# Attention output: one PSUM bank for both units of a pair, normalised between two VectorE transposes; the third group's evacuation on VectorE and four early score steps

## The chip, the cores and the metric

The kernel runs on one core of one Trainium2 chip. The metric is the device time of one execution in microseconds (us), lower is better; the time given is the median of several executions. Below, PE is TensorE, ACT is ScalarE, DVE is VectorE, POOL is GpSimd and SP is the queue that issues the DMAs.

## What is computed

A block on x of shape (2, 1024, 128): half a mixture-of-experts feed-forward (FFN), causal attention with 8 heads of 8 channels and l2-normalised queries and keys, and the same half FFN again.

```python
x = x + 0.5 * ffn(layernorm(x))     # 8 experts of 256 hidden, all computed for each token, summed, times a gate
x = x + attention(layernorm(x))
x = x + 0.5 * ffn(layernorm(x))

# attention
q, k, v = split(xn @ w_qkv)                       # (128, 192); 8 heads x 8 channels each
sim  = (l2norm(q) @ l2norm(k).T) * 8.0            # causal
o    = softmax(sim) @ v                           # (2, 8, 1024, 8)
out  = concat_heads(o) @ w_out                    # (64, 128)
```

## The kernel before

The 2,048 tokens are 4 groups of 512. Each engine has its own instruction list, written out by hand, and semaphores join them; nothing is reordered by a scheduler. There are three phases. Layer 0 (an FFN) handles the groups one after the other, 16 chunks of hidden units per group: per chunk PE makes three matmuls `up` (L443 to L449) and three `down` (L461 to L466), ACT a gelu (L765, L768), DVE the split into a high and a low part (L932, L934). Beside the chunks it makes the layer norm, q, k and v of the groups that are finished. Attention follows, then layer 1 (a second FFN).

**Attention** is 80 steps `s` in 40 quad steps `k` (a quad step is one block of keys for four heads; its two steps are two heads each). Per step PE makes the scores (L570) into one of `S_SETS` = 3 pairs of PSUM banks, ACT the exponentials (L778) into one of 8 slots, and POOL masks diagonal blocks (L1254). Per quad step PE then multiplies the probabilities with the values, `pv` (L591), `PV_LAG` = 3 quad steps later. So PE's list for quad step k is: scores 2k, scores 2k+1, pv(k-3), then at most one **job**. A score step waits until the exponentials that used its banks three steps before are done. Most steps hold 2x512 columns; the last of each unit holds 2x256.

A **unit** is (batch, query group, quad): 8 units of 3, 3, 7, 7, 3, 3, 7, 7 quad steps. `pv` adds a unit up in one PSUM bank, `output_bank(u)` = 7 or 6 in turn, as 4 heads x 32 rows (8 channels, the sum of the probabilities from a column of ones in `v_ones`, zeros) by 512 queries. The other of the two banks serves the **jobs** (`fill(n)` on PE writes it, `empty(n)` on DVE reads it): for each unit "rows" (DVE copies the bank to `oT`, L1076, PE transposes it in 4 tiles, L622, DVE divides by the sums, L1107 and L1109); for each second unit "features" (transposes back, L625, copy L1114) and "project" (times `w_out`, L628, added to x, L1118); and, for the fourth group, which the attention phase prepares itself, "ln" (L611), "qk" (L614), "v" (L617), "q_stack" and "k_stack" (L548). The next unit's first `pv` waits until the jobs in its bank are emptied.

The third group (p = 2) is prepared at the end of layer 0: in PE's chunks 12 and 13 of the last group stand the first score step, transposes (L414) and the products `qkv_products` (L538); ACT copies the second group's keys (L741), makes `xf` (L714), then the squares (L724) and the copies of q, k and v (L729, L734) and the FFN output `yT` (L788). The last unit's "rows", "features" and "project" stand in chunks 2, 4 and 6 of layer 1's first group.

## Time and profile before

| | |
|---|---|
| median of 3 executions | 298.76 us (298.69 to 298.80) |
| the profiled execution | 298.09 us, its span in the trace 296.4 us |
| PE matmuls busy | 280.2 us (95%) |
| ACT busy | 226.1 us (76%) |
| DVE busy | 216.8 us (73%) |
| POOL busy | 87.0 us (29%) |

Busy time is the union of an engine's instructions; matmuls are pipelined, so "busy" on PE holds overlaps, and the distance from one start to the next is what a matmul costs. Attention lies between about 118 and 197 us of the span, layer 0 before it and layer 1 behind it.

### The profile page before, as it was taken

What the parts mean: (1) busy time and instruction counts of PE and PEld (TensorE: products, weight loads), DVE (VectorE), ACT (ScalarE), POOL (GpSimd) and SP (SyncE); (2) the same over time, 40 slices, a digit from 0 to 9 for tenths busy, and PEclk for the clock granted to TensorE, in tenths of its full rate; (3) what the DMA queues carried; (4) which work ended last, traced back from release to release, by engine and by line L of the source; (5) the groups of instructions that cost most, each with busy time, mean ns of one, the idle gap of its engine ahead of it and who ended that gap; (6) DMA issues with size and microseconds to landing.
All of it is one profiled execution on the core that took longest, in us unless ns stands there. A gap on an engine that the chain in (4) does not pass through costs nothing.

```text
span 296.4 us, 5295 instructions
## 1 busy us (share of the span) xinstructions
PE 280.2 (95%) x1707; PEld 195.6 (66%) x1707; DVE 216.8 (73%) x567; ACT 226.1 (76%) x349; POOL 87.0 (29%) x151
## 2 busy tenths in 40 slices
PE   8898999999989988699989989899999999999995
PEld 8585788788778875143414433268888888888882
DVE  6799988979988886873593451148679797888675
ACT  2875877777877787999798899976677677687672
POOL 5333204204860680542137303212030310310010
PEclk9999999999999999899999999999999999999998
DMA  5710000000000000000000000000000100100101
GB/s 165 237 46 1 0 1 2 0 1 2 0 1 0 3 1 0 2 0 2 0 3 2 1 2 0 2 0 0 2 0 2 35 2 0 35 0 0 35 3 35
DMA packets 8060, 4.66 MB, mean 16 GB/s; under 512 B 642, under 2 KB 8036, under 8 KB 8036
## 3 DMA queue, kind: packets, MB, share of 16 engines
q1 hardware_dynamic: 8036, 4.35, 4.9%
q8 instruction: 13, 0.21, 0.3%
q14 instruction: 11, 0.09, 0.1%
HBM read 3.30 MB, written 1.05 MB: 15 GB/s over the span
## 4 chain that ended last, share of the span: by engine, by line
PE 69%; POOL 9%; ACT 7%; DVE 6%; issue 6%; SPq 1%; DMA 1%; DVEq 0%; POOLq 0%; ACTq 0%
PE ps L591 9%; PE ps L466 8%; PE ps L461 8%; PE ps L443 8%; PE ps L449 8%; PE ps L446 8%; PE ps L464 7%; ACT probs L778 3%; PE ps L570 3%; POOL rstd L1176 2%; PE ps L423 2%; PE ps L628 1%; PE ps L548 1%; PE ps L622 1%; DVE h_lo L934 1%
## 5 line engine op out<-in xcount | busy, mean ns | idle before, releaser
L765 ACT ACTIVATE h<-ps,cols 128x512 f32<-128x512 f32 x128 | 88.0, 690 | 50.5 <-PE ps L449 45.4
L934 DVE TENSOR_TENSOR h_lo<-h,h_hi 128x512 fp32r<-128x512 f32 x128 | 92.0, 724 | 29.0 <-ACT h_hi L768 26.0
L778 ACT ACTIVATE probs<-ps 128x1024 f32<-128x1024 f32 (+1 forms) x80 | 68.6, 962 | 6.1 <-PE ps L570 5.9
L461 PE MATMUL ps<-h_hi,w_hi 128*128 128x512 f32 x128 | 53.0, 414 | 0.3 <-DVE h_hi L932 0.3
L466 PE MATMUL ps<-h_lo,w_hi 128*128 128x512 f32 x128 | 50.9, 398 | 1.8 <-DVE h_lo L934 1.8
L443 PE MATMUL ps<-xT_hi,w_hi 128*128 128x512 f32 (+1 forms) x128 | 50.7, 396 | 0.3 <-ACT xT_hi L839 0.3
L449 PE MATMUL ps<-xT_lo,w_hi 128*128 128x512 f32 (+1 forms) x128 | 50.1, 391 | 0.0
L464 PE MATMUL ps<-h_hi,w_lo 128*128 128x512 f32 x128 | 50.0, 391 | 0.0
L446 PE MATMUL ps<-xT_hi,w_lo 128*128 128x512 f32 (+1 forms) x128 | 49.9, 390 | 0.0
L768 ACT ACTIVATE h_hi<-ps,cols 128x512 fp32r<-128x512 f32 x72 | 49.1, 682 | 0.0
L1254 POOL TENSOR_SCALAR_AFFINE_SELECT probs<-probs 128x256 f32<-128x256 f32 x64 | 26.4, 435 | 54.5 <-ACT probs L778 53.6
L591 PE MATMUL ps<-probs,v_ones 128*32 128x512 f32 (+3 forms) x384 | 40.2, 511 | 0.9 <-DVE x_sb L1118 0.5
L466 PEld LDWEIGHTS ps<-h_lo,w_hi 128*128 128x128 f32 x128 | 24.0, 188 | 9.9 <-DVE h_lo L934 4.8
L932 DVE CAST h_hi<-h 128x512 fp32r<-128x512 f32 x56 | 24.8, 443 | 7.1 <-ACT h L765 6.2
L443 PEld LDWEIGHTS ps<-xT_hi,w_hi 128*128 128x128 f32 x128 | 24.0, 188 | 5.8 <-ACT xT_hi L839 0.5
L461 PEld LDWEIGHTS ps<-h_hi,w_hi 128*128 128x128 f32 x128 | 24.1, 188 | 5.5 <-DVE h_hi L932 1.5
L449 PEld LDWEIGHTS ps<-xT_lo,w_hi 128*128 128x128 f32 x128 | 24.0, 188 | 5.5 <-DVE xT_lo L1129 0.2
L446 PEld LDWEIGHTS ps<-xT_hi,w_lo 128*128 128x128 f32 x128 | 24.0, 188 | 5.1
L464 PEld LDWEIGHTS ps<-h_hi,w_lo 128*128 128x128 f32 x128 | 24.2, 189 | 3.8
L570 PE MATMUL ps<-qT,kT 32*128 32x512 f16 (+3 forms) x192 | 20.0, 335 | 3.5 <-ACT probs L778 3.1
L570 PEld LDWEIGHTS ps<-qT,kT 32*128 32x128 f16 x192 | 5.7, 92 | 20.9 <-ACT probs L778 12.3
L1176 POOL TENSOR_TENSOR gate_rms<-gate_ms,neg_half 128x4 f32<-128x4 f32 x8 | 9.6, 1201 | 29.0 <-DVE gate_ms L899 29.0
(127 smaller groups left out, 301.4 us busy)
## 6 DMA issues: line engine op xcount, KB each, us to landing
w_raw<-in_L_ffn_w SPq DMA_DIRECT2D x8, 256.0 KB, 4.3
x_sb<-in_L_attn_x SPq DMA_DIRECT2D x3, 256.0 KB, 7.3
out_x<-x_sb SPq DMA_DIRECT2D x3, 256.0 KB, 2.3
x_sb<-in_L_attn_x SPq DMA_DIRECT2D x2, 128.0 KB, 2.1
out_x<-x_sb SPq DMA_DIRECT2D x2, 128.0 KB, 1.8
wqkv_sb<-in_L_attn_w_qkv SPq DMA_DIRECT2D x1, 96.0 KB, 6.7
wout_sb<-in_L_attn_w_out SPq DMA_DIRECT2D x1, 32.0 KB, 3.4
small<-in_L_ffn_b SPq DMA_DIRECT2D x1, 8.0 KB
```

The lines of the kernel that those rows point to most:

```text
L443: pe.matmul(bank, w1_hi[:, w], xT_hi[:, cols_g], start=True, stop=False)
L446: pe.matmul(bank, w1_lo[:, w], xT_hi[:, cols_g], start=False, stop=False)
L449: pe.matmul(bank, w1_hi[:, w], xT_lo[:, cols_g], start=False, stop=True).then_inc(up_done, 1)
L461: pe.matmul(y, w2_hi[:, w], h_hi[:, c % RING, :], start=(c == 0), stop=False)
L464: pe.matmul(y, w2_lo[:, w], h_hi[:, c % RING, :], start=False, stop=False)
L466: pe.matmul(y, w2_hi[:, w], h_lo[:, c % RING, :], start=False, stop=(c == CHUNKS - 1)).then_inc(down_done, 1)
L570: m = pe.matmul(ps[:, 2 * (s % S_SETS) + hd, at:at + width], kT[rows, st["quad"], k0:k0 + P], qT[rows, st["quad"], qc:qc + width], start=T ...
L591: m = pe.matmul(ps[ROW * j:ROW * j + ROW, bank, q0:q0 + width], v_ones[:, SEQ // P * st["b"] + kt, 4 * st["quad"] + j, :], probs[:, (s + j ...
L765: first = nc.scalar.activation(h[:, slot, :], ps[:, BANK_H + slot, :], ACT.Gelu, bias=bias)
L768: nc.scalar.activation(h_hi[:, slot, :], ps[:, BANK_H + slot, :], ACT.Gelu, bias=bias).then_inc(gelu_done, 1)
L778: nc.scalar.activation(probs[:, s % P_SLOTS, :, 0:width], ps[:, bank:bank + 2, 0:width], ACT.Exp, scale=SCALE).then_inc(exp_done, 1)
L934: dve.tensor_tensor(h_lo[:, slot, :], h[:, slot, :], h_hi[:, slot, :].bitcast(f32), ALU.subtract).then_inc(split_done, 1)
```

## The change

- **One bank for both units of a pair.** `v_ones` puts the second quad's channels and ones 16 columns further on (`SPREAD`), with zeros elsewhere, so both quads' `pv` add up in one bank: 16 rows for each of the 8 heads. There are 4 pairs instead of 8 units: quad steps 0-5, 6-19, 20-25, 26-39.
- **Normalising on DVE alone.** `output(pair)` makes a DVE transpose of 32x32 blocks out of the bank into `o_blocks`, a reciprocal, a product into `o_scaled`, and a second transpose into `o_feat`. The jobs "rows" and "features" are gone from PE. `wout_sb` gets 128 rows (zeros between the heads), loaded by 8 DMAs instead of 1, after a memset on POOL.
- **Jobs.** "project" is cut into two halves of 2 tiles; "qk" and "v" become two "qkv" jobs of 2 tiles and 192 columns. Their quad steps are set anew. In layer 1's first group "project" alone is left, in chunk 3.
- **The third group's evacuation**: copies of k of the second group, of q, k and v of the third, and the squares, move from ACT to DVE. In groups 1 and 2 ACT copies the values by four instructions instead of two.
- **Four early steps**: score steps 1, 2 and 3 stand in chunks 13, 14 and 15 of layer 0's last group (step 0 was in chunk 12 already); `score_set` gives steps 0 to 3 the banks 0 to 3 by turns. ACT makes the first two exponentials before `yT`.

```diff
-        u0, u1, u2, u3 = last_quad[0:4]
-        jobs = [(u0 + 1, "rows", 0), (u0 + 2, "q_stack", LAST - 1), (u0 + 3, "k_stack", LAST - 1),
-                (u1 + 1, "rows", 1), (u1 + 2, "features", 1), (u1 + 3, "project", 1),
-                (u1 + 4, "ln", LAST), (u1 + 5, "qk", LAST), (u1 + 6, "v", LAST), (u2 + 4, "rows", 2),
-                (u2 + 5, "q_stack", LAST), (u2 + 6, "k_stack", LAST)]
...
-        jobs.append((last_quad[4] + 2, "ffn_ln", 0))
...
-        jobs += [(quad_steps, "rows", u), (quad_steps, "features", u), (quad_steps, "project", u)]
+        jobs = [(q1, "ln", LAST), (q1 + 1, "project", (0, 0)), (q1 + 2, "project", (0, 1)),
+                (q1 + 5, "qkv", 0), (q1 + 6, "qkv", 1), (q1 + 7, "q_stack", LAST - 1), (q1 + 8, "k_stack", LAST - 1),
+                (q1 + 12, "q_stack", LAST), (q2 + 1, "k_stack", LAST),
+                (q2 + 4, "project", (1, 0)), (q2 + 5, "project", (1, 1)),
+                (q3 + 1, "project", (2, 0)), (q3 + 2, "project", (2, 1)), (q3 + 5, "ffn_ln", 0),
+                (quad_steps, "project", (pairs - 1, None))]
...
-        def output_bank(u):
-            return 7 - u % 2
+        def score_set(s):
+
+            return s % 2 if s < 4 else (s - 2) % S_SETS
+
+        def set_reader(s):
+
+            return s - 2 if s in (2, 3) else None if s == 4 or s < 2 else s - S_SETS
+
+        def output_bank(pair):
+            return 7 - pair % 2
...
-            sp.dma_start(wout_sb[:, :], w_out).then_inc(wout_in, 16)
+            sp.wait_ge(const_self, 6)
+            for head in range(HEADS):
+                row = ROW * (head % 4) + SPREAD * (head // 4)
+                sp.dma_start(wout_sb[row:row + HEAD_DIM, :], w_out[HEAD_DIM * head:HEAD_DIM * head + HEAD_DIM, :]).then_inc(wout_in, 16)
...
-                    if layer == 1 and first and c in (2, 4, 6):
-                        fill(len(jobs) - 4 + c // 2)
+                    if layer == 1 and first and c == 3:
+                        fill(len(jobs) - 1)
...
+                    if operands and last and c >= at["att_qkv"]:
+                        if c == at["att_qkv"]:
+                            pe.wait_ge(gelu_done, CHUNKS * GROUPS)
+                        scores(1 + c - at["att_qkv"])
...
-                if s >= S_SETS:
-                    pe.wait_ge(exp_done, s - S_SETS + 1)
+                if set_reader(s) is not None:
+                    pe.wait_ge(exp_done, set_reader(s) + 1)
...
+                opens, closes = st["first"] and st["quad"] == 0, st["last"] and st["quad"] == QUADS - 1
+                if opens and pair == 0:
                     pe.wait_ge(kT_done, LAST - 1)
-                if st["first"] and st["unit"] == 1:
+                if opens and pair == 1:
                     pe.wait_ge(resid, GROUP_TILES * GROUPS)
-                if st["first"] and st["unit"] > 1:
+                if opens and pair > 1:
                     pe.wait_ge(job_emptied, sum(at < k for at, *_ in jobs))
                 if st["diagonal"]:
...
-                                      start=(st["first"] and n == 0), stop=(st["last"] and n == len(st["item"]) - 1))
+                                      start=(opens and n == 0), stop=(closes and n == len(st["item"]) - 1))
...
                     pe.wait_ge(job_emptied, n)
+                if n == 0 or pair_of_job(n) != pair_of_job(n - 1):
+                    pe.wait_ge(o_copied, pair_of_job(n))
                 tiles = [slice(P * i, P * i + P) for i in range(GROUP_TILES)]
                 if kind in ("q_stack", "k_stack"):
                     pe.wait_ge(stack_done, 2 * arg + 2)
...
+                elif kind == "qkv":
+                    for i in halves[arg]:
+                        m = pe.matmul(bank[:, 192 * (i % 2):192 * (i % 2) + 192], xf[:, ATT, tiles[i]], wqkv_sb[:, :],
+                                      start=True, stop=True)
                 elif kind == "project":
-                    for tile in tiles:
+                    pair, half = arg
+                    pe.wait_ge(o_ready, pair + 1)
+                    for tile in tiles if half is None else [tiles[i] for i in halves[half]]:
...
-                        square_qk(g - 1)
-                        copy_qkv(g - 1)
+                        exp_scores(1)
...
+            def copy_k(p):
+                dve.wait_ge(stack_t, p + 1)
+                dve.tensor_copy(kT[:, :, GROUP * p:GROUP * p + GROUP],
+                                ps[:, BANK_KT, :].bitcast(f16).rearrange("p (a q) -> p a q", a=QUADS)).then_inc(kT_done, 1)
+
+            def copy_qkv(p):
+                dve.wait_ge(qkv_mm, p + 1)
+                dve.wait_ge(qkn_done, 2 * p)
+                halves_qkv = [ps[:, bank, 0:384].rearrange("p (t c) -> p t c", t=2) for bank in qkv_banks(p)]
+                for half, qkv in enumerate(halves_qkv):
+                    dve.tensor_copy(qk_raw[:, 2 * half:2 * half + 2, :], qkv[:, :, 0:2 * INNER])
+                for half, qkv in enumerate(halves_qkv):
+                    for quad in range(QUADS):
+                        last = dve.tensor_copy(v_of(slice(4 * p + 2 * half, 4 * p + 2 * half + 2), quad), v_columns(qkv, quad))
+                last.then_inc(qkv_copied, 1)
...
+                        copy_k(g - 2)
+                        copy_qkv(g - 1)
+                        own_squares(g - 1)
...
-                            copy_o(len(units) - 1)
-                        if c in (2, 4, 6):
-                            empty(len(jobs) - 4 + c // 2)
-                        if c == 7:
+                            output(pairs - 1)
+                        if c == 3:
...
-            def copy_o(u):
-                dve.wait_ge(pv_done, quads_until_unit[u])
-                if u:
-                    dve.wait_ge(job_filled, job_number["rows", u - 1] + 1)
-                dve.tensor_copy(oT[:, :], ps[:, output_bank(u), :]).then_inc(o_copied, 1)
+            def output(pair):
+
+                dve.wait_ge(pv_done, quads_until_unit[QUADS * pair + QUADS - 1])
+                dve.transpose(o_blocks[:, :, :].rearrange("p b r -> p (b r)"), ps[:, output_bank(pair), :]).then_inc(o_copied, 1)
+                dve.wait_ge(o_copied, pair + 1)
+                split_rows = o_blocks[:, :, :].rearrange("p b (q s) -> p b q s", q=QUADS)
+                dve.reciprocal(rden[:, :, :], split_rows[:, :, :, HEAD_DIM]).then_inc(rden_done, 1)
+                dve.wait_ge(rden_done, pair + 1)
+                if pair == 0:
+                    dve.wait_ge(o_zero, 1)
+                dve.tensor_tensor(o_scaled[:, :, :].rearrange("p b (q s) -> p b q s", q=QUADS)[:, :, :, 0:HEAD_DIM],
+                                  split_rows[:, :, :, 0:HEAD_DIM],
+                                  rden[:, :, :].unsqueeze(3).to_broadcast([P, BLOCKS, QUADS, HEAD_DIM]),
+                                  ALU.mult).then_inc(o_scaled_done, 1)
+                dve.wait_ge(o_scaled_done, pair + 1)
+                if pair:
+                    dve.wait_ge(job_filled, job_number["project", (pair - 1, 1)] + 1)
+                dve.transpose(o_feat[:, :], o_scaled[:, :, :].rearrange("p b r -> p (b r)")).then_inc(o_ready, 1)
 
...
+                elif kind == "qkv":
+                    dve.wait_ge(qkn_done, 2 * LAST)
+                    qkv = bank[:, 0:384].rearrange("p (t c) -> p t c", t=2)
+                    t0 = GROUP_TILES * LAST + halves[arg][0]
+                    dve.tensor_copy(qk_raw[:, halves[arg][0]:halves[arg][1] + 1, :], qkv[:, :, 0:2 * INNER])
+                    for quad in range(QUADS):
+                        last = dve.tensor_copy(v_of(slice(t0, t0 + 2), quad), v_columns(qkv, quad))
+                    last.then_inc(job_emptied, 1)
```

PE in layer 0's last group, from chunk 13's `down` on (L538 are the products for q, k and v, L570 before and L602 after the scores, L477 and L505 the transposes of `yT`). Before:

```order
L538 MATMUL ps<-wqkv_sb,xf 128x192 [waits qT_done,xf_done_att]
L538 MATMUL ps<-wqkv_sb,xf 128x192 x3
L461 MATMUL ps<-h_hi,w2_hi 128x512 [waits gelu_done]
L464 MATMUL ps<-h_hi,w2_lo 128x512
L466 MATMUL ps<-h_lo,w2_hi 128x512 [waits split_done]
L461 MATMUL ps<-h_hi,w2_hi 128x512 [waits h_hi_done]
L464 MATMUL ps<-h_hi,w2_lo 128x512
L466 MATMUL ps<-h_lo,w2_hi 128x512 [waits split_done]
L570 MATMUL ps<-qT,kT 128x512 [waits kT_done,gelu_done,wout_in,qT_done]
L570 MATMUL ps<-qT,kT 128x512
L477 MATMUL ps<-ident,yT 128x128 [waits qkv_copied,y_evac]
L477 MATMUL ps<-ident,yT 128x128 x3
L570 MATMUL ps<-qT,kT 128x384 [waits xf_done_ffn,y_evac,qkv_copied]
```

After (there L570 are the products for q, k and v, and L602 the scores):

```order
L602 MATMUL ps<-qT,kT 128x512 [waits gelu_done]
L602 MATMUL ps<-qT,kT 128x512
L489 MATMUL ps<-h_hi,w2_hi 128x512 [waits gelu_done]
L492 MATMUL ps<-h_hi,w2_lo 128x512
L494 MATMUL ps<-h_lo,w2_hi 128x512 [waits split_done]
L602 MATMUL ps<-qT,kT 128x384 [waits exp_done]
L602 MATMUL ps<-qT,kT 128x384
L602 MATMUL ps<-qT,kT 128x128 x2
L489 MATMUL ps<-h_hi,w2_hi 128x512 [waits h_hi_done]
L492 MATMUL ps<-h_hi,w2_lo 128x512
L494 MATMUL ps<-h_lo,w2_hi 128x512 [waits split_done]
L602 MATMUL ps<-qT,kT 128x384 [waits exp_done]
```

Score steps 1, 2 and 3 moved ahead of the `down` of chunks 14 and 15 and of the transposes of `yT`, steps 2 and 3 with a wait for exponentials 0 and 1.

DVE behind the gate of layer 0's last group (`ss`, `seed`, `rnorm` are the lengths of q and k; `x_sb<-ps,gate_half,x_sb` is the FFN's residual, which waits for the transposes of `yT`). Before:

```order
L923 RECIPROCAL gate_half<-gate_sum 128x4 [waits gate_ready]
L950 TENSOR_REDUCE ss<-sq 128x64 [waits newton_done,sq_done]
L957 TENSOR_SCALAR ss<-ss 128x64 [waits seed_done]
L959 TENSOR_SCALAR seed<-ss 128x64 [waits seed_done]
L964 TENSOR_SCALAR rnorm<-seed 128x64 [waits qkn_done,seed_done]
L942 SCALAR_TENSOR_TENSOR x_sb<-ps,gate_half,x_sb 128x128 [waits gate_ready,y_t]
```

After:

```order
L947 RECIPROCAL gate_half<-gate_sum 128x4 [waits gate_ready]
L993 COPY kT<-ps 128x2x512 [waits stack_t]
L1001 COPY qk_raw<-ps 128x256 [waits qkn_done,qkv_mm]
L1001 COPY qk_raw<-ps 128x256
L1004 COPY v_ones<-ps 128x2x4x8 x4
L1012 TENSOR_TENSOR sq<-qk_raw 128x512 [waits qkv_copied]
L974 TENSOR_REDUCE ss<-sq 128x64 [waits newton_done,sq_done]
L981 TENSOR_SCALAR ss<-ss 128x64 [waits seed_done]
L983 TENSOR_SCALAR seed<-ss 128x64 [waits seed_done]
L988 TENSOR_SCALAR rnorm<-seed 128x64 [waits qkn_done,seed_done]
L966 SCALAR_TENSOR_TENSOR x_sb<-ps,gate_half,x_sb 128x128 [waits gate_ready,y_t]
```

The copies `kT`, `qk_raw`, `v_ones` and the squares `sq` came in ahead of the lengths, and the residual stands behind all of them.

DVE in the attention phase, from the squares of the fourth group (`sq<-qk_raw`) on; `job_filled` is PE's fill of a job's bank. Before:

```order
L969 TENSOR_TENSOR sq<-qk_raw 128x512 [waits job_emptied]
L950 TENSOR_REDUCE ss<-sq 128x64 [waits newton_done,sq_done]
L957 TENSOR_SCALAR ss<-ss 128x64 [waits seed_done]
L959 TENSOR_SCALAR seed<-ss 128x64 [waits seed_done]
L964 TENSOR_SCALAR rnorm<-seed 128x64 [waits qkn_done,seed_done]
L311 TENSOR_TENSOR newton<-rnorm 128x64 [waits newton_done,seed_done]
```

After:

```order
L1012 TENSOR_TENSOR sq<-qk_raw 128x512 [waits job_emptied]
L974 TENSOR_REDUCE ss<-sq 128x64 [waits newton_done,sq_done]
L1143 COPY qT<-ps 128x2x512 [waits job_filled]
L981 TENSOR_SCALAR ss<-ss 128x64 [waits seed_done]
L983 TENSOR_SCALAR seed<-ss 128x64 [waits seed_done]
L988 TENSOR_SCALAR rnorm<-seed 128x64 [waits qkn_done,seed_done]
L1146 COPY kT<-ps 128x2x512 [waits job_filled]
L336 TENSOR_TENSOR newton<-rnorm 128x64 [waits newton_done,seed_done]
L338 TENSOR_TENSOR newton<-newton,ss 128x64 [waits newton_done]
```

The copies `qT` and `kT` of the third group's stacks, each with a wait for PE's fill, now stand between the fourth group's squares and its inverse lengths (`newton`); before, they stood ahead of these rows.

## Rows read from the trace of the kernel before

**Rows 1.** The page: busy time and share of the span, instructions.

```profile
PE 280.2 (95%) x1707; PEld 195.6 (66%) x1707; DVE 216.8 (73%) x567; ACT 226.1 (76%) x349; POOL 87.0 (29%) x151
```

**Rows 2.** Windows: stretch; PE, PEld, DVE, ACT, POOL busy; PE clock.

```profile
124.00:125.00 1.00, 1.00 (x12) 0.05 (x8) 0.86 (x5) 1.00 (x2) 1.00 (x2) 0.50 0.06 16
...
140.00:150.00 10.00, 9.78 (x94) 4.27 (x92) 6.09 (x20) 7.91 (x10) 1.76 (x5) 1.00 0.00 0
180.00:190.00 10.00, 9.30 (x92) 2.62 (x88) 1.43 (x4) 9.76 (x12) 1.46 (x4) 1.00 0.00 0
```

**Rows 3.** Waits over the span: us in total, times, longest.

```profile
ACT probs L778 <- PE ps L570: 5.9, 13, 0.9
```

**Rows 4.** ACT in order of time, exponentials merged: start, us, count, idle before.

```profile
120.69 4.75 ACT L778 ACTIVATE probs<-ps 128x1024 f32<-128x1024 f32 x6 [0.16 <-PE ps L570]
125.60 1.94 ACT L778 ACTIVATE probs<-ps 128x1024 f32<-128x1024 f32 x2 [0.17 <-PE ps L570]
...
140.64 1.08 ACT L778 ACTIVATE probs<-ps 128x512 f32<-128x512 f32 x2 [0.37 <-PE ps L570]
...
156.60 9.62 ACT L778 ACTIVATE probs<-ps 128x1024 f32<-128x1024 f32 x12 [0.86 <-PE ps L570]
...
181.04 12.09 ACT L778 ACTIVATE probs<-ps 128x1024 f32<-128x1024 f32 x14 [0.24 <-PE ps L570]
```

**Rows 5.** The chain that ended last: start, us, PE work.

```profile
62.59 1.30 PE ps L538 x8
...
129.73 0.59 PE ps L622 x4
...
139.29 1.08 PE ps L628 x8
...
143.50 1.09 PE ps L614 x8
...
145.92 1.05 PE ps L617 x8
...
158.11 0.34 PE ps L570 x8
158.45 1.00 PE ps L591 x16
```

**Rows 6.** ACT in order of time at the end of layer 0.

```profile
113.38 1.01 ACT L741 ACTIVATE kT<-ps 128x1024 f16<-128x1024 f16 x1
...
117.50 0.65 ACT L724 ACTIVATE sq<-ps 128x256 f32<-128x256 f32 x2
...
118.87 0.74 ACT L788 ACTIVATE yT<-ps,cols 128x512 f32<-128x512 f32 x1
```

**Rows 7.** DVE in order of time, idle time before in brackets.

```profile
118.18 0.69 DVE L950 TENSOR_REDUCE ss<-sq 128x64 f32<-128x512 f32 x1 [1.77 <-ACT sq L724]
...
200.32 0.67 DVE L1076 COPY oT<-ps 128x512 f32<-128x512 f32 x1
```

**Rows 8.** DVE groups by form: busy us, mean ns of one, idle before.

```profile
L1076 DVE COPY oT<-ps 128x512 f32<-128x512 f32 x8 | 5.4, 681 | 4.9 <-PE ps L591 4.8
...
L917 DVE RECIPROCAL logits<-gate_tanh 128x32 f32<-128x32 f32 x8 | 2.8, 353 | 0.3
...
L336 DVE TENSOR_TENSOR qkn<-qk_raw,rnorm 128x256 f32<-128x256 f32 x4 | 1.9, 524 | 0.3
```

**Rows 9.** Chain that ended last: DVE behind the "v" job.

```profile
147.34 0.69 DVE sq L969
...
154.24 0.62 DVE k_stack L353
```

**Rows 10.** PE in order of time in layer 1's first group.

```profile
201.09 0.39 PE L449 MATMUL ps<-xT_lo,w_hi 128*128 128x512 f32 x1
201.32 0.60 PE L622 MATMUL ps<-ident,oT 128*128 128x128 f32 x4
201.68 0.48 PE L461 MATMUL ps<-h_hi,w_hi 128*128 128x512 f32 x1
```

More of the change, by code:

```diff
@@ L232, in build @@
         SEED_OPS = 4
-        u0, u1, u2, u3 = last_quad[0:4]
-        jobs = [(u0 + 1, "rows", 0), (u0 + 2, "q_stack", LAST - 1), (u0 + 3, "k_stack", LAST - 1),
-                (u1 + 1, "rows", 1), (u1 + 2, "features", 1), (u1 + 3, "project", 1),
-                (u1 + 4, "ln", LAST), (u1 + 5, "qk", LAST), (u1 + 6, "v", LAST), (u2 + 4, "rows", 2),
-                (u2 + 5, "q_stack", LAST), (u2 + 6, "k_stack", LAST)]
-        for u in range(3, len(units) - 1):
-            at = last_quad[u] + 1
-            jobs.append((at, "rows", u))
-            if u % 2:
-                jobs += [(at + 1, "features", u), (at + 2, "project", u)]
@@ L246, in build @@
[L246 to L254 removed]
+        pairs = len(units) // QUADS
+        first_of_pair = [0] + [quads_until_unit[QUADS * i - 1] for i in range(1, pairs)]
@@ L261, in vector_rounds, with pair_of_job, v_part, v_of @@
+        def pair_of_job(n):
+            return steps[2 * min(jobs[n][0], quad_steps - 1)]["unit"] // QUADS
+        def v_part(quad):
+            return slice(SPREAD * quad, SPREAD * quad + HEAD_DIM)
+        def v_of(tiles, quad):
+            return v_ones[:, tiles, 4 * quad:4 * quad + 4, v_part(quad)]
         def vector_rounds(layer, c):
@@ L569, in scores @@
                         rows = slice(ROW * j, ROW * j + ROW)
-                        m = pe.matmul(ps[:, 2 * (s % S_SETS) + hd, at:at + width], kT[rows, st["quad"], k0:k0 + P],
+                        m = pe.matmul(ps[:, 2 * score_set(s) + hd, at:at + width], kT[rows, st["quad"], k0:k0 + P],
                                       qT[rows, st["quad"], qc:qc + width], start=True, stop=True)
@@ L818, in ffn_group @@
                             high_stacks(g - 2)
-                        if c == at["k_copy"]:
+                        if c == at["k_copy"] and not last:
                             copy_k(g - 2)
@@ L850, in _ @@
             ffn_groups(nc.scalar, 0, lambda g: ffn_group(0, g))
-            for s in range(1, len(steps)):
+            for s in range(2, len(steps)):
                 exp_scores(s)
@@ L1141, in _ @@
             inverse_lengths(dve, LAST - 1)
-            unit_vectors(dve, LAST - 1)
-            stacks(LAST - 1)
-            for n, (_, kind, arg) in enumerate(jobs[:-3]):
+            normalise(ATT, LAST, LAST)
+            for n, (at, kind, arg) in enumerate(jobs[:-1]):
+                if n == 0 or pair_of_job(n) != pair_of_job(n - 1):
+                    output(pair_of_job(n) - 1)
                 if kind == "ffn_ln":
                     normalise(FFN, GROUPS, 0)
-                if kind == "rows":
-                    copy_o(arg)
                 empty(n)
-                if (kind, arg) == ("rows", 0):
-                    normalise(ATT, LAST, LAST)
-                if kind == "v":
+                if kind == "ln":
+                    unit_vectors(dve, LAST - 1)
+                if (kind, arg) == ("project", (0, 1)):
+                    stacks(LAST - 1)
+                    dve.wait_ge(job_emptied, n + 1)
+                    first_stats(GROUPS)
+                if (kind, arg) == ("qkv", 1):
                     own_squares(LAST)
                     square_sums(LAST)
+                if (kind, arg) == ("q_stack", LAST - 1):
                     guesses(LAST)
+                if (kind, arg) == ("k_stack", LAST - 1):
                     inverse_lengths(dve, LAST)
```

127 lines of the change are left out of this document (55 added, 72 removed).

## Prediction

> **What bounds the kernel now.** I read the page first: PE is busy in 95% of the span [rows 1]. In the two FFN layers it is the limit. In attention that figure misleads, so I took windows there. The reader should compare two of them [rows 2]: from 180 to 190 us ACT is busy for 9.76 of 10 us, from 140 to 150 us for only 7.91, while PE shows 9.78. The table of waits says whom ACT's exponentials wait for: PE's scores, 5.9 us in total, 13 times, at most 0.9 us [rows 3]. ACT in order of time shows where: runs of exponentials with gaps of 0.17, 0.37, 0.86 and 0.24 us between them [rows 4].
>
> The two loads per quad step explain it. Units of seven quad steps hold 12 full and 2 half exponentials and take 12.09 us; a run of 8 full and 4 half takes 9.62 us [rows 4]. So a full one costs (2 x 12.09 - 9.62)/16 = 0.91 us, a half one 0.58 us, a full quad step 1.82 us of ACT. PE needs 0.34 us for its scores and 1.00 us for `pv` [rows 5], 1.34 us in all. With "rows" (0.59) it is 1.93, with "project" (1.08) 2.42 us [rows 5]. So ACT is the limit without a job and PE with one; several jobs in succession starve ACT, because the three score banks let PE run only 3 steps ahead.
>
> **The change part by part.**
>
> *PE in attention.* Gone: seven "rows" and three "features" fills, each four transposes; at 0.59 us [rows 5] they are 5.9 us. "qk" and "v" cost 1.09 + 1.05 us, the two new halves together what `qkv_products` cost, 1.30 us: 0.8 us less. Each "project" of 1.08 us becomes two of about 0.54 us [rows 5]. That is 6.7 us less work for PE, and no job of over 0.65 us is left. A full quad step then takes at most 1.34 + 0.65 = 1.99 us, and the score banks hold 2.73 us (three exponentials) against it: a step 0.2 us too long is repaid by the next one without a job. ACT is thus the limit nearly throughout, and the price of the removed jobs is not their 6.7 us but ACT's idle time, which I work out separately.
>
> *ACT's idle time.* From the end of exponential 7 (120.69 + 4.75 = 125.44) to the end of the last (181.04 + 12.09 = 193.13) are 67.69 us. The 72 exponentials in it are four runs of 12.09, one of 9.62, one of 1.94 and one of 1.08 us [rows 4], 61.00 us (the last unit's run of 12.09 stands for the four of its length). So 6.7 us are idle. I leave 0.8 us: about 0.3 for the stretch at half clock (below) and 0.5 for three tight places. Gain **5.9 us**. The tight places:
> - The fourth group's stacks. From the squares to the end of the stacks DVE took 154.24 + 0.62 - 147.34 = 7.5 us [rows 9]. Now two copies `qT` and `kT` (0.68 each, as the copy `oT` [rows 8]) with their waits for PE lie within, and the copies of the second half ahead of them: 0.8 + 7.5 + 1.4 and 0.6 of waiting, 10.3 us from the end of the second "qkv" fill. The fill "q_stack" six quad steps later comes up after ten full and two half exponentials, 10.3 us, less 0.3 since PE waits for ACT at other points of the two steps. So PE may wait 0.3 us there, against a reserve of 2.73 - 1.34 = 1.4 us before ACT notices.
> - `pv` that opens a pair waits for the jobs in its bank: now twice instead of six times, and the last job before it is emptied in half the time.
> - `output(pair)` on DVE: transpose 0.68, reciprocal 0.35, product 0.52, transpose 0.68, 2.2 us [rows 8]. Its reader, "project", stands at least two quad steps (3.6 us) later, so it is covered; it would have to take over 3.5 us to be seen.
>
> *The price of a DVE transpose* has no row before. From below the copy of the same 128x512 out of PSUM, 0.68 us [rows 8], since all elements have to pass; from above two such passes, 1.36 us. I take 0.68: copies, casts and products of this size all take one pass here, and a transpose moves the same elements. The other end is the second rival. The Trainium skill ("VectorE: DVE Perf Modes", The three transpose paths) gives 311 ns for 128x128 in 16 bits; four times that is 1.24 us for the width here, an estimate from the page; by it the total would be about 291.2 us. No row of before shows one.
>
> *The end of layer 0.* ACT loses the copy `kT` and the squares and copies of q, k and v. The first began at 113.38 and moves 1,024 elements as an exponential does (0.91), the others took 118.87 - 117.50 = 1.37 us up to `yT` [rows 6]. Together 2.3 us. ACT will then wait for PE's transposes ahead of `xf` instead; I take 0.3 us off for that. The early scores 1 to 3 keep ACT fed while `yT` is transposed. So exponential 6, which began at 125.44 - 2 x 0.91 = 123.6, begins near 121.6: **2.0 us**. DVE takes the work over: `kT` 0.68, two copies of q and k and four small ones, about 1.7 us. It was free from 118.18 - 1.77 = 116.4 on [rows 7] and will be done near 118.7 with `kT` ahead of them, about when `yT` is, which the transposes need as well (it began at 118.87 behind ACT's copies [rows 6] and will begin near 118.1). Queued behind are squares, lengths, the residual and the fourth group's norm, all about 0.6 us later than now; POOL waits for that norm ahead of its masks 6 and 7. The next `pv` wait for those masks some 1 us behind that, and ACT has two exponentials in hand; without that cover, what DVE is late is late on the path.
>
> *Layer 1.* PE is the limit. One matmul follows the other after 0.23 us (201.32 - 201.09), and the fill "rows" moves the next by 201.68 - 201.32 = 0.36 us [rows 10]; "features" is as long: **0.7 us**. "project" stays, one chunk (1.37 us, six matmuls of 0.23) behind 201.32, at 202.7; `output(3)` starts at 200.3 where `oT` did [rows 7] and is ready at 202.5. Four DVE instructions in a row delay the splits, but PE takes them three chunks later.
>
> *At nothing:* seven more DMAs and their wait on SP are issued while nothing but x and weights for later is pending; the smaller memsets lie under the first loads; two more small ACT copies in groups 1 and 2 lie under PE's work with three chunks of reserve. From above I allow 0.5 us for them together.
>
> **Sum.** 5.9 + 2.0 + 0.7 = 8.6 us. The profiled execution took 298.09 us (span 296.4 and 1.7 around it): 289.5. The median lies 0.67 us above it: **290.2 us**.
>
> **The rivals.**
> - *ACT still waits* (0.22). The DVE chain of the tight places, or PE's, is late by more than its reserve at the pair boundaries, and 2 to 3 us of the 6.7 stay. For it: DVE has one job list, and everything behind a waiting instruction waits. Against: it has 3.9 us in 10 free [rows 2]. 290.2 + 2.3 = 292.5 us.
> - *The transpose costs twice as much* (0.10). In attention it stays covered (3.5 us). In layer 1 "project" becomes ready at 200.3 + 2 x 1.36 + 0.87 = 203.9, and PE, which is there at 202.7, stands still for 1.2 us: 291.4 us.
> - *The gaps are not PE's jobs* (0.04). If ACT waited for something else, the change would do only its two ends, 2.7 us: 296.1 us. Against it stand [rows 3] and the 180 to 190 window.
> - *PE's clock falls, and the kernel gets slower* (0.03). PE has idle pieces in each quad step once ACT is the limit. The granted clock was 0.50 (1.2 GHz) in the microsecond from 124, behind a stretch in which PE had waited for ACT again and again; half clock came here once [rows 2]. At half clock a quad step costs PE 2 x 1.34 = 2.68 us against ACT's 1.82, 0.86 us more. All 40 steps: 290.2 + 34 = 324 us; from 10 steps on the gain is gone. Against it: from 180 to 190 us, with no jobs but one and PE waiting for ACT, the clock stayed at 1.00 [rows 2]. The Trainium skill ("TensorE: Matmul & The Clock Gate", A second HAM failure mode: psum-queue depth-cycling) says that many short idle times between groups of matmuls made one kernel's clock swing; by that rule this rival would be the likely one, and this trace disagrees.
>
> **How the numbers follow.** The forecast has 0.58, all idle time gone (below 289.5) 0.03. The likeliest case reaches from 289.1 (everything that is idle gone) to 291.2 (0.5 for what I put at nothing, 0.5 more idle). The range also takes in the second rival and the half of the first: 289.0 to 292.7. Within 0.2% (0.6 us) is what a measurement can't tell from no change. Faster 0.96, same 0.01, slower 0.03.
>
> **What would show it.** After the change: no transposes of `oT` and `o_tok` on PE; ACT busy over 9.5 of 10 us in all windows from 122 to 185; the wait of exponentials for scores under 1.5 us; the last exponential's end near 185 instead of 193.1; exponential 6 starting near 121.6; STREAM_TRANSPOSE near 0.68 us; PE's busy share in attention down while its clock is 1.00. I am wrong if ACT shows gaps at the pair boundaries, if the transposes of `yT` wait for DVE's copies, or if the clock is low over several quad steps.

## The result and the profile after

The changed kernel takes **288.69 us** (median of 4 executions, 288.29 to 288.86) against 298.78 for the kernel before on the same chip (4 executions, 298.69 to 299.05): a ratio of 0.9659, 95% interval 0.9642 to 0.9676. On another chip it was 288.74 against 299.07, 0.9663 (0.9639 to 0.9687). It is faster, by 1.5 us more than the 290.2 forecast, and just below the range's lower end of 289.0. The profiled execution took 288.67 us, its span 286.9.

The page, against [rows 1]: PE lost 6.0 us of busy time, ACT 3.3.

```profile
PE 274.2 (96%) x1651; PEld 191.6 (67%) x1651; DVE 216.9 (76%) x573; ACT 222.8 (78%) x346; POOL 87.6 (31%) x155
```

The windows of attention (stretch; PE, PEld, DVE, ACT, POOL busy; PE's granted clock), against [rows 2]:

```profile
120.00:130.00 10.00, 8.75 (x94) 2.85 (x96) 5.86 (x25) 10.00 (x14) 6.59 (x16) 1.00 0.01 2
130.00:140.00 10.00, 9.47 (x88) 3.05 (x80) 6.79 (x16) 9.85 (x13) 3.75 (x8) 1.00 0.01 2
140.00:150.00 10.00, 10.00 (x108) 3.96 (x104) 6.83 (x26) 10.00 (x12) 1.58 (x4) 1.00 0.01 2
150.00:160.00 10.00, 9.09 (x118) 3.48 (x114) 7.23 (x16) 9.63 (x13) 8.15 (x19) 1.00 0.00 1
160.00:170.00 10.00, 9.93 (x96) 3.64 (x94) 3.39 (x7) 10.00 (x13) 1.74 (x6) 1.00 0.01 2
170.00:180.00 10.00, 9.40 (x92) 3.01 (x88) 3.83 (x8) 9.93 (x13) 2.57 (x7) 1.00 0.01 2
```

ACT is busy for 59.4 of 60 us. ACT in order of time (start, us, count, idle before), against [rows 4, 6]:

```profile
113.70 0.78 ACT L739 ACTIVATE xf<-ps,cols 128x512 f32<-128x512 f32 x1 [0.22 <-PE ps L442]
...
116.01 1.92 ACT L803 ACTIVATE probs<-ps 128x1024 f32<-128x1024 f32 x2
118.56 0.69 ACT L813 ACTIVATE yT<-ps,cols 128x512 f32<-128x512 f32 x1 [0.63 <-PE ps L494]
119.15 35.44 ACT L803 ACTIVATE probs<-ps 128x1024 f32<-128x1024 f32 x42
154.96 29.87 ACT L803 ACTIVATE probs<-ps 128x512 f32<-128x512 f32 x36 [0.37 <-PE ps L602]
```

Of the listed gaps between the runs of exponentials one of 0.37 us is left; the list holds no pause under 0.15 us. The 9.5 us that the span lost (296.4 to 286.9) split into three stretches:

- **Up to exponential 7's end.** Exponentials 2 to 7 take 4.75 us in one run, as in [rows 4], so 7 ends at 119.15 + 4.75 = 123.90, before at 125.44: **1.54 us** (2.0 forecast).
- **From there to the last exponential's end.** 154.96 + 29.87 = 184.83, so 60.93 us instead of 67.69: **6.76 us** (5.9 forecast).
- **Behind it.** 286.9 - 184.83 = 102.07 instead of 296.4 - 193.13 = 103.27: **1.20 us** (0.7 forecast).

DVE's groups by form: both transposes take 0.71 us, nearly what the copy of that size did (0.68, [rows 8]).

```profile
L1135 DVE STREAM_TRANSPOSE o_feat<-o_scaled 128x512 f32<-128x512 f32 x4 | 2.8, 711 | 0.1
L1121 DVE STREAM_TRANSPOSE o_blocks<-ps 128x512 f32<-128x512 f32 x4 | 2.8, 710 | 4.3 <-PE ps L625 4.2
L1128 DVE TENSOR_TENSOR o_scaled<-o_blocks,rden 128x256 f32<-128x256 f32 x4 | 1.7, 424 | 0.1
L1124 DVE RECIPROCAL rden<-o_blocks 128x32 f32<-128x32 f32 x4 | 1.4, 354 | 0.1
```

The one gap stands at the job "q_stack" of the fourth group. PE in order of time there:

```profile
152.21 1.07 PE L625 MATMUL ps<-probs,v_ones 128*32 128x384 f32 x16
154.09 0.61 PE L580 MATMUL ps<-ident,q_stack 128*128 128x128 f16 x8 [0.81 <-DVE k_stack L378]
154.63 0.29 PE L602 MATMUL ps<-qT,kT 32*128 32x256 f16 x4
```

And DVE, from the fourth group's last stack on:

```profile
153.32 0.62 DVE L378 TENSOR_TENSOR k_stack<-qkn,k_stack 128x256 f16<-128x256 f32 x1
154.74 0.69 DVE L1143 COPY qT<-ps 128x1024 f16<-128x1024 f16 x1 [0.79 <-PE ps L580]
```

PE has been done with `pv` since 153.28 and waits 0.81 us for DVE's stack, which ends at 153.94.

### The profile page after: what moved, and what is told of

Its sections match the earlier page's. It is cut to its first block, busy times and chain, and to the rows that moved or that the text cites. A ratio compares the mean times of both kernels' runs of the same rounds, so it can differ in the third digit from the quotient of the medians.

```text
span 286.9 us, 5191 instructions
## 1 busy us (share of the span) xinstructions
PE 274.2 (96%) x1651; PEld 191.6 (67%) x1651; DVE 216.9 (76%) x573; ACT 222.8 (78%) x346; POOL 87.6 (31%) x155
## 4 chain that ended last, share of the span: by engine, by line
PE 73%; POOL 8%; ACT 8%; issue 5%; DVE 4%; DVEq 0%; POOLq 0%; ACTq 0%
PE ps L494 9%; PE ps L489 9%; PE ps L471 8%; PE ps L477 8%; PE ps L474 8%; PE ps L492 8%; PE ps L625 8%; ACT probs L803 5%; PE ps L602 3%; PE ps L664 2%; PE ps L656 2%; PE ps L451 2%; PE ps L580 2%; PE ps L442 2%; POOL rstd L1231 1%
## 5 line engine op out<-in xcount | busy, mean ns | idle before, releaser
L803 ACT ACTIVATE probs<-ps 128x1024 f32<-128x1024 f32 (+1 forms) x80 | 67.0, 1013 | 0.6 <-PE ps L602 0.4
L477 PE MATMUL ps<-xT_lo,w_hi 128*128 128x512 f32 (+1 forms) x128 | 50.0, 391 | 0.0
L625 PE MATMUL ps<-probs,v_ones 128*32 128x512 f32 (+3 forms) x384 | 38.8, 495 | 0.0
L477 PEld LDWEIGHTS ps<-xT_lo,w_hi 128*128 128x128 f32 x128 | 24.0, 188 | 5.5 <-DVE xT_lo L1182 0.2
L602 PE MATMUL ps<-qT,kT 32*128 32x512 f16 (+3 forms) x192 | 21.3, 329 | 2.9 <-ACT probs L803 2.3
L602 PEld LDWEIGHTS ps<-qT,kT 32*128 32x128 f16 x192 | 6.5, 91 | 25.2 <-ACT probs L803 15.1
L1231 POOL TENSOR_TENSOR gate_rms<-gate_ms,neg_half 128x4 f32<-128x4 f32 x8 | 10.6, 1320 | 28.5 <-DVE gate_ms L923 28.5
(130 smaller groups left out, 288.4 us busy)
```

The lines of the kernel that those rows point to most:

```text
L477: pe.matmul(bank, w1_hi[:, w], xT_lo[:, cols_g], start=False, stop=True).then_inc(up_done, 1)
L602: m = pe.matmul(ps[:, 2 * score_set(s) + hd, at:at + width], kT[rows, st["quad"], k0:k0 + P], qT[rows, st["quad"], qc:qc + width], start=T ...
L625: m = pe.matmul(ps[ROW * j:ROW * j + ROW, bank, q0:q0 + width], v_ones[:, SEQ // P * st["b"] + kt, 4 * st["quad"] + j, :], probs[:, (s + j ...
L803: nc.scalar.activation(probs[:, s % P_SLOTS, :, 0:width], ps[:, bank:bank + 2, 0:width], ACT.Exp, scale=SCALE).then_inc(exp_done, 1)
```

## The experiments

Ten kernels on three chips, the kernel before timed beside each. On the first chip (pairs only, head only, no early steps, a third exponential) it took 299.13 us, on the second (more PE work, double transposes, later job, both) 299.51, on the third (fills in layer 1, the changed kernel again) 299.07.

**1. The pair's bank and DVE's normalising alone** (`pairs_only`): the changed kernel with the end of layer 0 as before.

```diff
-                            pe.wait_ge(gelu_done, CHUNKS * GROUPS)
-                        scores(1 + c - at["att_qkv"])
...
-                        exp_scores(1)
+                        square_qk(g - 1)
+                        copy_qkv(g - 1)
...
-                        copy_k(g - 2)
-                        copy_qkv(g - 1)
-                        own_squares(g - 1)
                         square_sums(g - 1)
```

> The changed kernel with its part at the end of layer 0 undone: ACT again copies the second group's kT and squares and copies the third group's q, k and v, and only score step 0 is early. The shared bank, the DVE transposes, the new jobs and layer 1 stay. My theory (the attention phase was held up by ACT's idle time, 6.7 us between the end of exponential 7 and the last, and layer 1 gives 1.2 us on its own): 298.8 - 7.9 = 290.9 us, exponential 6 starts at 123.6 as before the change, and from the end of exponential 7 to the last exponential's end stay about 61.1 us. Rival (the early start is what keeps PE ahead of ACT, so the two parts need each other): more than 1.5 us of ACT's idle time comes back and the time is over 292 us.

Measured: 291.33 us, ratio 0.9737 (0.9707 to 0.9767). ACT in order of time:

```profile
120.95 4.75 ACT L802 ACTIVATE probs<-ps 128x1024 f32<-128x1024 f32 x6 [0.16 <-PE ps L598]
126.49 30.81 ACT L802 ACTIVATE probs<-ps 128x1024 f32<-128x1024 f32 x36 [0.79 <-PE ps L598]
157.66 29.87 ACT L802 ACTIVATE probs<-ps 128x512 f32<-128x512 f32 x36 [0.36 <-PE ps L598]
```

The gaps of [rows 4] go with this part alone: 1.15 us of listed idle time is left, 0.79 of it in a stretch in which PE had half its clock (last section). The theory's 290.9 is nearer than the rival's 292; the two parts don't need each other for ACT's idle time to go.

**2. The end of layer 0 alone** (`head_only`): the kernel before with the copies and squares on DVE and the early steps.

```diff
+                        scores(1 + c - at["att_qkv"])
...
-                        square_qk(g - 1)
-                        copy_qkv(g - 1)
+                        exp_scores(1)
...
+                        copy_k(g - 2)
+                        copy_qkv(g - 1)
+                        own_squares(g - 1)
```

> The kernel before with the part at the end of layer 0 alone: DVE makes the evacuation of the third group, score steps 1 to 3 are early; units, PE transposes and jobs as before. My theory (the parts add up): exponential 7 ends about 1.6 us earlier than before (125.4), ACT's idle time of 6.7 us stays, total 298.8 - 1.6 = 297.2 us. Rival (PE is the limit in attention as it stood, so an earlier ACT only waits more): under 0.6 us gained, 298.3 us or more, with the wait of the exponentials for scores grown from 5.9 to over 7 us.

Measured: 297.93 us, ratio 0.9966 (0.9947 to 0.9986), between theory and rival by the medians. In the trace the start is won, and then most of it is lost again. The table of waits (us, times, longest) and the first runs of exponentials:

```profile
ACT probs L787 <- PE ps L582: 6.9, 12, 1.1
```

```profile
119.29 4.74 ACT L787 ACTIVATE probs<-ps 128x1024 f32<-128x1024 f32 x6
124.77 4.75 ACT L787 ACTIVATE probs<-ps 128x1024 f32<-128x1024 f32 x6 [0.74 <-PE ps L582]
130.06 9.59 ACT L787 ACTIVATE probs<-ps 128x1024 f32<-128x1024 f32 x10 [0.53 <-PE ps L582]
```

Exponential 7 ends at 124.03 instead of 125.44, 1.4 us earlier, but the waits grow from 5.9 [rows 3] to 6.9 us. While PE's jobs set the pace, an earlier ACT mostly waits longer. By the medians this part is worth 299.13 - 297.93 = 1.2 us alone, and 291.33 - 288.69 = 2.6 us on top of the other. Both figures hold a share of the clock. The spans of the two profiles, each with one half-clock stretch in attention, differ by only 0.3 us (296.4 and 296.1): the rival's "under 0.6 us gained". Most executions of the kernel before had a lower mean clock than the profiled one (last section), and all ten of this kernel a higher one. Of the 2.6 us, 1.8 are the earlier end of exponential 7 (125.70 to 123.88), and the rest is about what the 0.79 us gap costs, which the changed kernel's profile does not have.

**3. No early steps** (`no_early`): the changed kernel with score steps 1 to 3 where they were before (step 1 behind the last `down`, steps 2 and 3 behind the transposes of `yT`), and `yT` ahead of exponential 1.

```diff
-                            pe.wait_ge(gelu_done, CHUNKS * GROUPS)
-                        scores(1 + c - at["att_qkv"])
...
-                        exp_scores(1)
```

> The changed kernel with score steps 1 to 3 back behind layer 0's last chunk (three pairs of score banks in turn from step 0 on); DVE keeps the evacuation. Theory A (the early steps feed ACT, as my prediction had it): exponential 2 starts later than 119.15, and the time is 0.8 to 1.5 us above the changed kernel's 288.7. Theory B (read from the trace of the changed kernel: its scores stand ahead of the last two downs, so ACT waits 0.63 us for yT; without them downs, yT and its transposes are all earlier): exponential 2 starts near 118.9, and the time is 288.4 us, the same or slightly less.

Measured: 289.36 us, ratio 0.9681 (0.9654 to 0.9708), 0.7 us above the changed kernel: just under my range, but not the rival's 288.4. The trace shows less: from the start of `xf` to the end of exponential 7 are 10.32 us against 10.19, and the pause of 0.37 us (listed as 0.18) that ACT has later lies in a half-clock stretch. So the early steps are worth 0.1 to 0.7 us; what DVE's evacuation is worth by itself no run shows.

**4. A third exponential ahead of `yT`** (`exp2_first`), where the changed kernel's ACT waits 0.63 us for the last `down`.

```diff
                         exp_scores(1)
+                        exp_scores(2)
```

> The changed kernel with the third exponential ahead of yT on ACT, in the 0.63 us in which ACT waits for the last down. Theory (ACT's list is what counts from here on): exponential 3 starts at 119.4 instead of 120.06, exponential 4 right behind it, the wait of 0.63 us is gone; 288.7 - 0.6 = 288.1 us. Rival (yT 0.25 us later makes its transposes, the banks 4 and 5 of step 4 and the residual late): ACT waits before exponential 4 for what it gained, 288.7 us.

Measured: 288.35 us, ratio 0.9641 (0.9615 to 0.9667). It lies between theory and rival. The 0.63 us are filled; a wait of 0.23 us for scores appears ahead of exponential 4. In the trace, `xf` to the end of exponential 7 takes 9.78 us instead of 10.19, 0.4 us less. The medians are 0.34 to 0.4 us apart, which the executions by themselves (288.02 to 288.75, against 288.29 to 288.86) would not show.

**5. More work for PE** (`pe_more4`): four transposes that nobody reads ahead of each of the six half projections in attention (six times 0.59 us of busy time; from their start to the half projection's are only 0.50 us, 3.0 us in all).

```diff
+                    if half is not None:
+                        for i in range(4):
+                            pe.transpose(bank[:, tiles[i % 4]], ident[:, :], ident[:, :])
```

> The changed kernel with four more fp32 transposes of the identity on PE ahead of each of the six half projections in attention (0.59 us each time, 3.5 us in all, as much as six of the ten fills that the change removed; their result is overwritten). My theory (ACT is the limit and three score banks give PE a reserve of about 1.4 us): two such steps in a row exceed a quad step of ACT by 2 x 0.65 = 1.3 us, so ACT notices little: 288.7 + 0 to 0.6 us. Rival (each us of PE's work in attention counts): 288.7 + 3.5 = 292.2 us.

Measured: 290.99 us, ratio 0.9716 (0.9684 to 0.9749), 2.3 us more, between the two. PE in order of time at the first pair of halves, and ACT's waits for scores:

```profile
135.47 0.65 PE L657 MATMUL ps<-ident 128*128 128x128 f32 x4
135.97 0.61 PE L659 MATMUL ps<-wout_sb,o_feat 128*128 128x128 f32 x4
136.51 0.40 PE L602 MATMUL ps<-qT,kT 32*128 32x384 f16 x8
```

```profile
ACT probs L806 <- PE ps L602: 2.6, 8, 0.8
```

The longest, 0.79, is in a half-clock stretch; the others add up to 1.8 us, against the changed kernel's 0.37. So at least 1.4 us of the 3.0 show: a step with 0.50 + 0.54 us of jobs is too long when the next one has the same. The theory's "0 to 0.6 us" was too low, the rival's 3.5 too high. Two jobs in succession eat the reserve, as the prediction read in the trace of before.

**6. Double transposes** (`double_tr`): each DVE transpose made twice, 0.71 us more each.

```diff
+                dve.transpose(o_again[:, :], ps[:, output_bank(pair), :])
                 dve.transpose(o_blocks[:, :, :].rearrange("p b r -> p (b r)"), ps[:, output_bank(pair), :]).then_inc(o_copied, 1)
```

> The changed kernel with each DVE transpose made twice (the first one into a buffer that nobody reads), 8 more of 0.71 us, 5.7 us more for DVE. My theory: in attention they are covered (half projections two quad steps later), and in layer 1 PE, which reached the projection at 194.3 when o_feat was ready at 194.3, waits 1.4 us: 288.7 + 1.4 to 1.7 = 290.2 us. Rival (DVE's list is tight in attention too, since the fourth group's stacks stand behind it): over 1 us of gaps between exponentials, 291.5 us or more.

Measured: 290.91 us, ratio 0.972 (0.9688 to 0.9752), 2.2 us more. The table of waits:

```profile
PE ps L657 <- DVE o_feat L1138: 1.9, 2, 1.2
ACT probs L804 <- PE ps L603: 1.6, 5, 0.4
```

PE stands still for 1.2 us ahead of layer 1's "project", the figure of the prediction's second rival to the tenth, and for 0.7 us ahead of one in attention, which the theory here had as covered. The changed kernel has neither: what the transposes really cost is hidden, but with 0.7 us to spare, not with the 1.3 that the prediction's 3.5 against 2.2 us meant (2.3 + 1.4 of chain less 0.7 of waiting is 3.0 us of cover).

**7. "q_stack" one quad step later** (`q_later`).

```diff
-                (q1 + 12, "q_stack", LAST), (q2 + 1, "k_stack", LAST),
+                (q1 + 13, "q_stack", LAST), (q2 + 1, "k_stack", LAST),
```

> The changed kernel with the job that transposes the fourth group's q_stack one quad step later (19 instead of 18). In the changed kernel ACT's only gap between exponentials, 0.37 us at 154.6, lies where PE waited for DVE's stacks. Theory (that wait is the gap): the gap is gone, 288.7 - 0.35 = 288.3 us. Rival (the gap only moves to the opening of the next pair or to the k_stack job): 288.7 us.

Measured: 288.72 us, ratio 0.9643 (0.9615 to 0.9672), no different from the changed kernel in the median, as the rival had it. ACT:

```profile
124.23 60.61 ACT L803 ACTIVATE probs<-ps 128x1024 f32<-128x1024 f32 x72 [0.79 <-PE ps L602]
```

The 0.37 us gap is gone and none comes in its place, so the wait for the stack was its cause; 72 exponentials without a listed gap take 60.61 us. But this execution had the half-clock stretch, with a gap of 0.79 us that the changed kernel's profile does not have. Four of the five executions had a mean clock of 0.990 to 0.993 and took 288.64 to 288.96 us; the fifth had 0.996 and took 287.85.

**8. Both** (`both`): edits 4 and 7 together.

> The changed kernel with both: exponential 2 ahead of yT, and q_stack one quad step later. If each is worth what its own theory says and they add: 288.7 - 0.6 - 0.35 = 287.75 us. If either rival holds, 288.1 or 288.35 us.

Measured: 287.93 us (287.40 to 288.18), ratio 0.9621 (0.9594 to 0.9649): faster than the changed kernel by 0.8 us in the medians, the fastest here.

**9. Fills in layer 1** (`l1_fills`): eight fills of four transposes that nobody reads, in chunks 4 to 11 of layer 1's first group.

```diff
+                    if layer == 1 and first and 4 <= c < 12:
+                        for i in range(GROUP_TILES):
+                            pe.transpose(ps[:, 6, P * i:P * i + P], ident[:, :], ident[:, :])
```

> The changed kernel with eight dummy fills (four transposes of the identity matrix each, into a bank that nobody reads afterwards) behind chunks 4 to 11 of layer 1's first group, where PE is the limit and where the removed fills stood. My theory: an interruption of the FFN's stream costs not only the 0.36 us up to the next matmul, but 0.45 us, since that first matmul keeps PE longer than 0.23 us: 8 x 0.45 = 3.6 us, 292.3 us by the median of 288.7. Rival, the term as the prediction had it: 0.36 us each, 2.9 us, 291.6 us. In the trace, the stretch from the first up to the second group's first up tells them apart best.

Measured: 292.55 us, ratio 0.979 (0.9759 to 0.9821), 3.8 us more. PE in order of time, one chunk:

```profile
197.72 0.39 PE L471 MATMUL ps<-xT_hi,w_hi 128*128 128x512 f32 x1
...
198.41 0.60 PE L531 MATMUL ps<-ident 128*128 128x128 f32 x4
198.77 0.48 PE L489 MATMUL ps<-h_hi,w_hi 128*128 128x512 f32 x1
199.08 0.40 PE L492 MATMUL ps<-h_hi,w_lo 128*128 128x512 f32 x1
199.32 0.40 PE L494 MATMUL ps<-h_lo,w_hi 128*128 128x512 f32 x1
199.55 0.40 PE L471 MATMUL ps<-xT_hi,w_hi 128*128 128x512 f32 x1
```

A chunk with a fill takes 199.55 - 197.72 = 1.83 us, one without 1.36. So a fill costs 0.47 us here (0.47 in six of the eight chunks, 0.44 in two): 0.36 until the next matmul starts, and that one keeps PE for 0.31 instead of 0.23 us.

**10. The changed kernel again** (`after_again`).

> The changed kernel itself once more. My theory: the half-clock stretch at the layer change comes and goes between executions of one kernel, and is not a matter of the version; where it shows, ACT has a gap of up to 0.8 us near exponential 8 and the execution is 0.5 us or more longer. So the median stays near 288.7 (288.3 to 289.2). Rival: the changed kernel's order keeps the clock up, then no execution of it shows the stretch and the times lie within 0.3 us of each other.

Measured: 288.74 us; five executions of 288.37, 289.31, 288.74, 288.95 and 288.73, with a mean clock of 0.997, 0.990, 0.999, 0.991 and 0.991. They differ by 0.9 us, not by the rival's 0.3. Its profile shows no half-clock stretch in attention. That the executions of 289.31 and 288.95 us had one is likely by their clock, and not shown; the third with a low clock, 288.73, was no slower than the one of 0.999.

## Why the prediction was right in its mechanism, and where its sum was short

**What bounds the kernel: right.** ACT sets the pace of attention once PE's jobs are smaller. Experiment 1 removes the gaps with the jobs alone, and experiment 5 brings some back with PE work alone. ACT's busy share, its last end (184.83, "near 185" forecast) and PE's clock came as described. One sign did not: PE's busy share in attention went up, to 56.6 of the 60 us above from 55.6 in the same six windows before, since PE lost less work (6.0 us in the whole span) than attention lost time (6.76 + 1.54 us). The third and the fourth rival did not come true: all of ACT's listed waits there are for PE's scores, and in this profile the clock stayed at 1.00 in attention though PE waited for ACT again and again (15.1 us over 27 of its score steps).

**ACT's idle time, 5.9 forecast, 6.76 measured: the step that failed, by its size.** "I leave 0.8 us" was 0.43 too much: the tight places cost 0.37 instead of 0.5, and the 0.3 for the half-clock stretch did not come in this execution. The other 0.4 us lie in "61.00 us": I added the lengths of seven runs, each of which holds the end of a last exponential that overlaps the next in one long run. 72 in a run take 60.6.

The distances from start to start show more. Where ACT has its scores in time, a full exponential starts the next after 0.904 us and a half one after 0.477. The run of 12.09 us is 12 x 0.904 + 2 x 0.477 = 11.80 us by its starts, and the pauses under 0.15 us are in no list. Counted this way ACT was held up for 8.5 us between exponentials 7 and 79 before (the prediction's 6.7) and for 1.7 us after (its 0.8). So both figures were too low, by 1.8 and by 0.9 us, and the difference is the miss. Of the 1.7 us, 0.56 are the stack's, and 0.35 each stand ahead of exponentials 26 and 66, behind two half exponentials. All three are waits for PE's scores, and the last two are there in every experiment. So ACT is not quite the limit throughout.

**The tight places.** The place was right, the sum a coincidence of two errors. DVE's chain from the squares to the stacks ran from 144.71 to 153.94, 9.2 us, near what was worked out (8.9 and 0.6 of waiting); PE waited 0.81 us instead of 0.3. And the reserve "of 1.4 us" left out that the fill itself comes behind the wait: with the 0.54 us from its start to the next scores (154.09 to 154.63), 1.35 us are spent, and ACT notices 0.37 of them, though that is within the reserve as I had counted it. Experiment 7 shows the cause. `pv` at a pair's opening caused no gap. `output(pair)` took 2.3 us (2.2 forecast).

**The end of layer 0, 2.0 forecast, 1.54 measured.** `xf` began 0.58 us earlier (114.28 to 113.70): the copy `kT` (0.90 from its start to that of `xf`) less 0.32 of waiting, of which the row lists 0.22. Of the 1.37 us of squares and copies ACT lost 0.63 again, as it waits for the last `down` ahead of `yT`; the prediction named no such wait, since it looked at the transposes behind `yT` and not at PE in front of it. Before, PE's scores had also held exponential 2 back by 0.16 us, and that went. DVE's copies were done at 117.6 and held nobody. The figure of 1.54 is uncertain by some tenths: in the profiles of the changed kernel and of the experiments with the same layer 0, `xf` starts anywhere from 113.2 to 113.8 us, and in experiment 10's profile exponential 7 ends at 123.6, 1.85 us earlier than before. Experiment 2 adds what the prediction did not say: most of this gain holds only beside the other one.

**Layer 1, 0.7 forecast, 1.20 measured: mis-sized.** I read the price of a fill up to the start of the next matmul (0.36). That matmul is longer too, and the trace of before had it: a chunk with "rows" took 202.46 - 200.64 = 1.82 us against 1.37.

```profile
200.64 0.39 PE L443 MATMUL ps<-xT_hi,w_hi 128*128 128x512 f32 x1
...
202.46 0.39 PE L443 MATMUL ps<-xT_hi,w_hi 128*128 128x512 f32 x1
```

Experiment 9 confirms it with 0.44 to 0.47 us, eight times over. Two fills are 0.9 us. "project" took 0.20 us less as well (0.89 us up to the next matmul instead of 1.09); it now reads 128 rows instead of 64, and why that is quicker I did not try. Before, and then after:

```profile
207.77 1.16 PE L628 MATMUL ps<-wout_sb,o_feat 64*128 64x128 f32 x8
208.86 0.50 PE L461 MATMUL ps<-h_hi,w_hi 128*128 128x512 f32 x1
```

```profile
194.45 1.13 PE L656 MATMUL ps<-wout_sb,o_feat 128*128 128x128 f32 x8
195.34 0.48 PE L489 MATMUL ps<-h_hi,w_hi 128*128 128x512 f32 x1
```

**At nothing: right.** 6.76 + 1.54 + 1.20 leave nothing of the 9.5 us for more DMAs, memsets or copies.

**The offset of 0.67 us** from the profiled execution to the median was carried over as if it belonged to the kernel. It belongs to that execution: the profiled 298.09 is near the lower end of 33 executions of the kernel before on these chips (298.05 to 299.88). It goes with the clock: the profiled one had a mean clock of 0.991, as had the 7 of the 33 that took 298.05 to 298.57; the other 26 had 0.985 to 0.987 and took 298.65 to 299.88. The changed kernel's profiled execution lies 0.02 us under its median, and none of its 9 has a clock under 0.990. So about 0.7 of the 10.1 us between the medians comes on top of what the two profiles show, and the parts of the change explain only the 9.4 us between those.

**The first rival** (ACT still waits, 292.5) did not come true, nor did **the second**; experiment 6 shows that its mechanism and its price in layer 1 were right, had the transpose cost twice as much. My estimate of 1.24 us for a width of 512 was four times the figure that the Trainium skill ("VectorE: DVE Perf Modes", The three transpose paths) gives for 128x128 in 16 bits; measured are 0.71 us for 128x512 in 32 bits, so it was the multiplying that did not hold, and the page's own figure no run here shows.

In sum the misses are +0.86 (ACT), -0.46 (head), +0.50 (layer 1) and +0.65 (offset): 1.55 us, of the 1.5 observed. That they add up so well is in part luck, since the head alone is uncertain by 0.3 us.

## What to carry to other kernels

When one engine's jobs starve the engine that sets the pace, the price of a job is the idle time it causes there, and a gain elsewhere (an earlier start) pays only once that idle time is gone: by the traces it was 0.3 us alone and 1.8 us behind the other part. Read the cost of an interruption from period to period (chunk to chunk), not up to the next instruction's start. Measure how long an engine was held up from start to start, since lengths of runs hide overlaps and short pauses. And before carrying the distance between a profile and a median over to another kernel, look at how far executions of one kernel lie apart, and at their clock.

## What was not expected of the hardware

**Half clock, off and on.** Right behind the change of layer PE had a granted clock of 0.50 for 3.4 us in the profiles of before and of experiments 1, 2, 3, 5, 6, 7 and 8, and not in those of the changed kernel (twice), 4 and 9. Up to 130 us experiments 5, 6, 7 and 9 are the changed kernel, instruction for instruction, and three of them have it. So the version alone does not decide it. How often it comes may still depend on the version: the lowest mean clocks, 0.985 to 0.987, came in 26 of 33 executions of the kernel before, in 2 of 4 of experiment 1, which has its layer change too, in 1 of 5 of experiment 3, and in no other. What those executions did differently no profile shows; in experiment 1 they were no slower (291.09 and 291.27 us against 291.39 and 291.41). Windows of experiment 7, in which it came early:

```profile
120.00:121.00 1.00, 0.28 (x4) 0.13 (x2) 0.97 (x5) 1.00 (x3) 0.85 (x3) 0.90 0.00 0
121.00:122.00 1.00, 1.00 (x8) 0.30 (x10) 0.97 (x7) 1.00 (x3) 1.00 (x4) 0.50 0.00 0
122.00:123.00 1.00, 1.00 (x8) 0.00 (x0) 0.90 (x7) 1.00 (x2) 0.83 (x3) 0.50 0.06 16
123.00:124.00 1.00, 1.00 (x12) 0.14 (x8) 0.90 (x4) 0.43 (x1) 1.00 (x3) 0.50 0.00 0
```

In the first microsecond PE was busy for 0.28 of it. What it costs goes with when it begins. In experiments 1, 2, 5 and 7 it began 2.2 to 2.7 us ahead of the end of exponential 7, and ACT's gap before exponential 8 was 0.74 to 0.79 us. In experiments 6 and 8 and in the kernel before it began 1.5 to 1.7 us ahead, and the gap was 0.35, 0.23 and 0.17. In experiment 3 it began 1.1 us ahead, and the one gap of 0.18 stands before exponential 10. The four executions of experiment 9 fall into two pairs: 292.09 and 292.11 us with a mean clock of 1.000, 293.00 and 293.08 with 0.994.

The prediction says that half clock "came here once". The trace of before shows it twice: also in the last 3.8 us of the span, as every profile here does in its last 1.4 to 4.4 us. So a mean clock of 0.997, as in experiment 10's profile, is no sign of the stretch at the layer change.

**A DVE transpose** of 128x512 in 32 bits takes 0.71 us, out of PSUM and out of SBUF alike, against 0.68 for the copy of that size.
